# Graph network of four layers: TensorE drains carry three kinds of signals, and the step to the next block of nodes moves to the heads of the passes

## The chip, the cores and the metric

The kernel runs on one core of a Trainium2 chip. The metric is the time of one execution on the device, in microseconds (us), as a median of runs. A profiled execution of the kernel before is at hand as well. A core has TensorE (PE, matmuls; PEld is its loading of weights), VectorE (DVE), ScalarE (ACT), GpSimd (POOL) and SyncE (SP, which here only issues DMAs). Each works through its own list of instructions in order, and they wait for one another by semaphores.

## The reference

6,250 nodes with 64 features each go through four layers over the same 200,000 edges (sorted by destination). Each layer takes the normed and rectified features `h` of the nodes and adds its result to `x`.

```python
h = relu(layernorm(x));  x = x + L0(h, edge_attr, src, dst, W, b)
    # msg = [h[src], edge_attr];  agg = segment_sum(msg, dst);  relu([h, agg] @ W.T + b)
h = relu(layernorm(x));  x = x + L1(...)
    # pre = h[src] @ W_q + h[dst] @ W_k + edge_attr @ W_e;  score = leaky(pre) @ a_w
    # softmax of the scores over each dst;  segment_sum(alpha * (h[dst] @ W_v), dst)
h = relu(layernorm(x));  x = x + L2(...)
    # segment_sum(h[src] * weight, dst)
h = relu(layernorm(x));  x = x + L3(...)
    # attention by relation and rule: q of dst, keys of src; softmax over each dst; segment_sum
```

## The kernel before

The edges are 392 batches of 512 (4 tiles of 128). Each layer is one pass over the batches: `sum0` (layer 0, from about 120 to 2330 us), `score1` (layer 1, 2400 to 4966), `sum2` (layer 2, 4990 to 5665) and `attention3` (layer 3, 5790 to 8236). Between them stand the phases `head`, `middle1`, `middle2`, `middle3` and `end3`, which work on nodes, not on edges. Each pass and each phase is a block of its own with a barrier of all engines behind it (`Phase`, its end at L224, L227 and L230).

In a pass each engine runs its own `pipeline(eng, [(lag, stage), ...])`: in each step it does the listed stages in the order of the list, each for the batch that lies `lag` behind. So the order on an engine is fixed, and an engine that waits in one stage holds up all stages behind it. `done(eng, s, b)` waits until semaphore `s` has counted batch `b`, and `free(eng, s, b, ring)` until it has counted the batch that used the same slot before.

GpSimd gathers the rows of the source nodes by four indirect DMAs for each batch (`gather_stage`, L801) in `sum0` (table `node_rows`; for one batch in eight the rows come from TensorE lookups instead), `score1` (`src_rows`) and `attention3` (`rel_rows`). `sum2` has no gathers: it reads rows that `score1` kept in memory. The gathered rows lie in 8 slots (`ROW_RING`). A slot comes free in `sum0` by `s_sum` (TensorE's sum of the batch, L1119), in `score1` by `s_pre` (VectorE's `join`, L1512).

The stages that the change touches:
- `sum0`, TensorE `sums` (L1119): four matmuls add the rows of a batch into a bank, and the last of them signals `s_sum`. VectorE's `add` (L1168), VectorE's `build` (L1158), ScalarE's `join` (L1080) and GpSimd's gathers wait for it. The lookups (`lookups`, L1127) signal `s_used_dve` and `s_used_act` by their matmuls; VectorE (L1199) and ScalarE (L1097) wait for them.
- `score1`, TensorE `look` (L1488 and L1493) waits for VectorE's `hot` (L882), for `s_score` (VectorE's `scores`, L1527) and for the edge features, and signals `s_looked`. VectorE's `join` (L1512) and SyncE's next loads (L1446) wait for it.
- `score1`, TensorE `spread` (L1390) waits for `s_diag` (ScalarE, L1399) and signals `s_spread`, for which VectorE's `maxima` (L1539) and ScalarE's `spread_stage` (L1399) wait.

```python
pipeline(pe, [(1, look), (6, spread)])
pipeline(dve, [(7, maxima), (4, join), (9, sums), (7, running), (4, leak),
               (7, tops), (0, hot), (7, biases), (4, scores)])
```

VectorE's `scores` is last in its step and TensorE's `look` of the next step waits for a `scores` one step back. Nodes are treated in windows of 128. A pass stands in a loop over windows that here runs once (all instruction counts are 392 or multiples). Behind each pass, a phase `<name>_next` steps `dst_rel`, `dst_pairs`, `window_lane` and `base` to the next window (L910, L915, L918, L934), and the phases between the layers set them back (`reset_windows`, L906, and the copies at L1948, L1950 and L2006).

## Time and profile before

| | |
|---|---|
| runs | 8364.23 us median of 3 (8340.83 to 8364.46) |
| profiled execution | 8303.98 us, span in the trace 8301.9 us |
| busy in the span | PE 62%, PEld 45%, VectorE 55%, ScalarE 51%, GpSimd 60% |
| `sum0`, 120 to 2330 us | 5.6 us for a batch |
| `score1`, 2400 to 4966 us | 6.5 us for a batch |
| `sum2`, 4990 to 5665 us | 1.7 us for a batch |
| `attention3`, 5790 to 8236 us | 6.2 us for a batch |

No engine is busy for much over 60% of the span. The rows below are from the same execution; "idle before" is the time in which an engine stood still ahead of an instruction, and the name behind the arrow is what the profile takes to have ended it ("remote" is a semaphore for which it names no instruction, "issue" is no wait that it shows).

### The profile page before, as it was taken

How to read it: one execution, taken by the hardware profiler on the slowest of the kernel's cores; microseconds unless marked ns; L12 is line 12 of the kernel's file. 1: busy time of each engine (PE TensorE's matmuls, PEld its weight loads, DVE VectorE, ACT ScalarE, POOL GpSimd, SP SyncE). 2: the span in 40 equal slices, each digit the busy share in tenths (PEclk: the TensorE clock that was granted, in tenths of full speed). 3: DMA queues.
4: the chain of work that ended last, by engine and by line, in shares of the span. 5: the costliest groups of instructions: out<-in, count | busy, mean ns of one | idle time of the engine just before them, and what ended most of it. 6: DMA issues, size and time to landing. Idle time of an engine off the chain costs nothing. (4 is left out here: it accounts for less than half of the span.)

```text
span 8301.9 us, 160097 instructions
## 1 busy us (share of the span) xinstructions
PE 5143.2 (62%) x38193; PEld 3732.4 (45%) x38194; DVE 4604.7 (55%) x21263; ACT 4230.9 (51%) x11643; POOL 4975.0 (60%) x5713
## 2 busy tenths in 40 slices
PE   4666666666664444444444458997666666666665
PEld 3555556555552222222222227885444444444443
DVE  5555545555544444444444458996555555555556
ACT  3555555555524444444444448994555555555554
POOL 5555555555536556665655648994566666666563
PEclk8888888888876666766666669998666666666666
DMA  4333323233334444444444447885222222222221
GB/s 117 92 90 89 89 81 95 83 89 88 89 88 134 132 130 133 133 132 132 135 132 130 133 110 238 268 267 206 59 64 65 62 65 64 65 64 64 63 65 42
DMA packets 673099, 908.82 MB, mean 109 GB/s; under 512 B 141462, under 2 KB 430216, under 8 KB 672729
## 3 DMA queue, kind: packets, MB, share of 16 engines
q1 hardware_dynamic: 502654, 605.53, 23.2%
q0 software_dynamic: 168944, 301.30, 15.0%
q8 instruction: 42, 0.69, 0.0%
q14 instruction: 102, 0.84, 0.0%
q10 hardware_dynamic: 1357, 0.47, 0.0%
HBM read 696.57 MB, written 210.28 MB: 109 GB/s over the span
## 5 line engine op out<-in xcount | busy, mean ns | idle before, releaser
L801 POOL DMA_INDIRECT rows<-src_rows,idx_slots x1531 | 1488.2, 972 | 1009.8 <-issue 505.5
L801 POOL DMA_INDIRECT rows<-rel_rows,idx_slots x1531 | 1455.2, 950 | 941.6 <-issue 377.6
L801 POOL DMA_INDIRECT rows<-node_rows,idx_slots x1339 | 1281.4, 957 | 935.2 <-PE bank L1119 342.9
L1399 ACT ACTIVATE onehot<-ident,fresh_slots 128x128 f32<-128x128 f32 x3136 | 998.9, 390 | 1090.5 <-remote 787.6
L1390 PE MATMUL bank<-onehot,ones 128*128 128x512 f32 x1568 | 1279.6, 912 | 4.8 <-ACT onehot L1399 4.8
L1488 PE MATMUL bank<-w_e,edge_in 128*128 128x256 f32 x784 | 410.4, 622 | 1334.0 <-remote 693.2
L1097 ACT ACTIVATE dst_pairs<-pre,minus_node 128x512 bf16<-128x512 int16 x816 | 578.6, 720 | 1096.6 <-remote 649.3
L1488 PEld LDWEIGHTS bank<-w_e,edge_in 128*128 128x128 f32 x784 | 187.0, 285 | 1763.2 <-issue 1173.0
L1127 PE MATMUL bank<-by_chunk,dst_pairs 128*128 128x192 bf16 x6144 | 776.7, 269 | 322.7 <-issue 239.7
L1539 DVE CUSTOM_DVE_ANT_0 onehots<-bank,onehots 128x512 f32<-128x512 f32 x392 | 271.0, 691 | 1132.2 <-remote 823.1
L1127 PEld LDWEIGHTS bank<-by_chunk,dst_pairs 128*128 128x128 bf16 x6144 | 581.8, 108 | 408.8 <-issue 291.6
L1127 PE MATMUL bank<-wide_room,dst_pairs 128*128 128x192 bf16 x3264 | 476.4, 279 | 454.0 <-ACT dst_pairs L1101 303.7
L1696 PE MATMUL bank<-rows,onehot 128*128 128x65 f32 x3136 | 595.5, 351 | 239.5 <-DVE wide_room L1793 179.7
L1199 DVE TENSOR_SCALAR dst_pairs<-pre,node_at 128x512 bf16<-128x512 int16 x1536 | 534.5, 348 | 277.9 <-remote 156.0
L1696 PEld LDWEIGHTS bank<-rows,onehot 128*128 128x128 f32 x3136 | 547.7, 263 | 266.6 <-issue 249.5
L1636 ACT ACTIVATE shrink<-grown 128x1 f32<-128x1 f32 x392 | 80.0, 204 | 1103.0 <-DVE grown L1741 554.2
L1168 DVE TENSOR_TENSOR wide_room<-bank,wide_room 96x128 f32 x392 | 112.3, 286 | 816.4 <-remote 564.4
L1127 PEld LDWEIGHTS bank<-wide_room,dst_pairs 128*128 128x128 bf16 x3264 | 309.6, 110 | 535.8 <-ACT dst_pairs L1101 341.9
L1101 ACT ACTIVATE dst_pairs<-dst_pairs,ones 128x512 bf16<-128x512 bf16 x816 | 542.2, 709 | 1.6
L1651 ACT ACTIVATE onehot<-onehots,edge_in 128x128 f32<-128x128 bf16 x1568 | 503.1, 392 | 19.9
L1318 ACT ACTIVATE onehot<-onehots,edge_scale 128x128 f32<-128x128 bf16 x1568 | 503.0, 392 | 11.6 <-DVE onehots L1373 11.4
L1471 ACT ACTIVATE onehot<-onehots,exp_bias 128x512 bf16<-128x512 f32 x392 | 283.7, 724 | 428.9 <-DVE max_by_chunk L1569 198.8
(309 smaller groups left out, 12039.1 us busy)
## 6 DMA issues: line engine op xcount, KB each, us to landing
edge_in<-dst_line SPq DMA_DIRECT2D x392, 256.0 KB
spill<-rows SPq DMA_DIRECT2D x392, 256.0 KB
rows<-spill SPq DMA_DIRECT2D x392, 256.0 KB, 3.1
hot_rows<-rows SPq DMA_DIRECT2D x98, 712.0 KB
onehots<-hot_rows SPq DMA_DIRECT2D x196, 356.0 KB, 3.5
onehots<-src_low SPq DMA_DIRECT2D x98, 512.0 KB
edge_in<-in_ea_l SPq DMA_DIRECT2D x98, 256.0 KB
edge_in<-in_eaT_l SPq DMA_DIRECT2D x392, 64.0 KB
```

What stands on the lines that cost most here:

```text
L801: pool.indirect_dma_start(out=to[:, b.slot(ROW_RING), g, :], out_offset=None, in_=table, in_offset=bass.IndirectOffsetOnAxis(ap=idx[:, col ...
L1097: act.activation(act_hots[:, n % 2, :], look_in(b), ACT.Square, bias=minus_node[:, n:n + 1]).then_inc(s_square, 1)
L1101: act.activation(act_hots[:, n % 2, :], act_hots[:, n % 2, :], ACT.Relu, scale=-1.0, bias=ones[:, 0:1])\
L1127: last = pe.matmul(look_banks(b)[g // 2][:, at:at + PARTS * D], hot[:, g * P:(g + 1) * P], node_parts(j), start=(j == 0 and g % 2 == 0), s ...
L1199: dve.tensor_scalar(dve_hots[:, n % 4, :], look_in(b), node_at[:, n:n + 1], None, ALU.is_equal)\
L1318: last = act.activation(onehot[:, b.slot(RING), g, :], plain_of(b)[:, g, :], ACT.Copy, scale=edge_scale[:, b.slot(RING), g:g + 1])
L1390: return pe.matmul(bank, ones[:, :], diag[:, b.slot(2), :, :].rearrange("p g e -> p (g e)"), start=start, stop=True)
L1399: last = act.activation(diag[:, b.slot(2), g, :], ident[:, :], ACT.Copy, scale=fresh_slots[:, b.slot(2 * RING), g:g + 1])
L1471: act.activation(exp_out, masked1[:, b.slot(2), :], ACT.Exp, bias=exp_bias[:, slot, :], accum_out=exp_sum[:, slot, :])
L1488: pe.matmul(to, edge_blocks[:, b.slot(RING), :], w1_e[:, :, :].rearrange("p g f -> p (g f)"), start=True, stop=False)
L1651: last = act.activation(weighted[:, b.slot(2), g, :], onehot_b[:, b.slot(ONEHOT_RING), g, :], ACT.Copy, scale=share[:, b.slot(RING), g:g + 1])
L1696: last = pe.matmul(summed, weighted[:, b.slot(2), g, :], rows[:, b.slot(ROW_RING), g, D:2 * D + 1], start=(g == 0), stop=(g == TILES_PER_B ...
```

## The change

Two things are changed. First, at three places the last matmul of a stage no longer carries the signal: a `drain` of TensorE stands behind it and carries it. These are `sums` of `sum0`, `look` of `score1` and `spread` of `score1`, 392 each, 1176 in all. The signals of the lookups in `sum0`, and all of `sum2` and `attention3`, stay on matmuls. Second, the four phases `<name>_next` are gone, and their steps stand at the head of each pass on VectorE (`next_window`). So that the first step gives the first window, the start values are set one window back (`dst_rel` plus 128, `window_lane` and `base` minus 128), and `reset_windows` has three instructions in place of five. TensorE waits for the stepped `base` ahead of its pipeline in `score1` and `attention3`. The diff, cut:

```diff
--- before.py
+++ after.py
@@ -658,10 +658,13 @@
                 c.do(dve.tensor_reduce(n_windows[:, :], base[:, :], AX, ALU.max))
                 c.do(dve.tensor_single_scalar(n_windows[:, :], n_windows[:, :], 1, ALU.add))
                 dve.wait_ge(s_local, 1)
-                dve.tensor_copy(dst_rel[:, :], dst_rel0[:, :]).then_inc(s_set, 1)
-                dve.tensor_copy(base[:, :], base0[:, :]).then_inc(s_set, 1)
+                dve.tensor_single_scalar(dst_rel[:, :], dst_rel0[:, :], float(WINDOW), ALU.add)\
+                   .then_inc(s_set, 1)
+                dve.tensor_single_scalar(base[:, :], base0[:, :], -WINDOW, ALU.add)\
+                   .then_inc(s_set, 1)
                 dve.wait_ge(s_const, 14)
-                dve.tensor_copy(window_lane[:, :], lane[:, :]).then_inc(s_set, 1)
+                dve.tensor_single_scalar(window_lane[:, :], lane[:, :], float(-WINDOW), ALU.add)\
+                   .then_inc(s_set, 1)
                 dve.wait_ge(s_set, 3)
 
                 dve.wait_ge(s_w, 16 * (len(weight_loads) + 3 + TILES_PER_BATCH))
@@ -894,16 +897,14 @@
                                ACT.Copy, scale=-FAR_BELOW, bias=FAR_BELOW).then_inc(s_far, 1)
             return fars
 
-        n_reset = 5
+        n_reset = 3
 
         def reset_windows(pool, s_set):
 
-            for n, (to, of) in enumerate(((dst_rel[:, :], dst_rel0[:, :]),
-                                          (dst_pairs[:, :, 0], dst_rel0[:, :]),
-                                          (dst_pairs[:, :, 1], dst_rel0[:, :]),
-                                          (window_lane[:, :], lane[:, :]),
-                                          (base[:, :], base0[:, :]))):
-                pool.tensor_copy(to, of).then_inc(s_set, 1)
+            for n, (to, of, by) in enumerate(((dst_rel[:, :], dst_rel0[:, :], float(WINDOW)),
+                                              (window_lane[:, :], lane[:, :], float(-WINDOW)),
+                                              (base[:, :], base0[:, :], -WINDOW))):
+                pool.tensor_single_scalar(to, of, by, ALU.add).then_inc(s_set, 1)
                 pool.wait_ge(s_set, n + 1)
 
         def next_places(dve, c):
@@ -918,21 +919,19 @@
             c.do(dve.tensor_single_scalar(window_lane[:, :], window_lane[:, :], float(WINDOW),
                                           ALU.add))
 
-        def windows_loop(name, sweep, steps):
+        def next_window(dve, s_stepped, s_based, steps):
+
+            c = Chain(dve, s_stepped)
+            for step in steps:
+                step(dve, c)
+            dve.tensor_scalar(base[:, :], base[:, :], WINDOW, LAST_BASE, ALU.add,
+                              ALU.min).then_inc(s_based, 1)
+            dve.wait_ge(s_based, 1)
+
+        def windows_loop(sweep):
             windows = nc.values_load(n_windows[0:1, 0:1], min_val=1, max_val=N_PAD // WINDOW + 1)
             with nc.Fori(0, windows):
                 sweep()
-                with Phase(nc, name + "_next") as ph:
-                    s = ph.sem("set")
-                    block = ph.open()
-
-                    @block.vector
-                    def _(dve):
-                        c = Chain(dve, s)
-                        for step in steps:
-                            step(dve, c)
-                        c.do(dve.tensor_scalar(base[:, :], base[:, :], WINDOW, LAST_BASE,
-                                               ALU.add, ALU.min))
 
         def sum_sweep(name):
 
@@ -1116,10 +1116,10 @@
                             done(pe, s_joined, b)
                             free(pe, s_added, b, 2)
                             for g in range(TILES_PER_BATCH):
-                                last = pe.matmul(sum_bank(b), sum_rows[:, b.slot(ROW_RING), g, :],
+                                pe.matmul(sum_bank(b), sum_rows[:, b.slot(ROW_RING), g, :],
                                                  onehots_of(b)[:, g, :],
                                                  start=(g == 0), stop=(g == TILES_PER_BATCH - 1))
-                            last.then_inc(s_sum, 1)
+                            pe.drain().then_inc(s_sum, 1)
 
                         def look_up(b, hot, j):
                             for g in range(TILES_PER_BATCH):
@@ -1213,6 +1213,7 @@
                                     bank[:, 0:2 * PARTS * D].rearrange(
                                         "p (g n d) -> p g d n", n=PARTS, d=D), AX)
                             last.then_inc(s_filled, 1)
+                        next_window(dve, s_stepped, s_based, [next_places])
                         c = Chain(dve, s_parts)
                         for tiles in src_groups:
                             value = of_tiles(normed, tiles)
...
@@ -1490,18 +1494,20 @@
                                       start=True, stop=False)
                             for g in range(TILES_PER_BATCH):
                                 for n, part in enumerate(parts):
-                                    last = pe.matmul(
+                                    pe.matmul(
                                         to[:, g * D:(g + 1) * D],
                                         onehotT[:, b.slot(ONEHOT_RING), g, :], part, start=False,
                                         stop=(g == TILES_PER_BATCH - 1 and n == PARTS - 1))
-                            last.then_inc(s_looked, 1)
+                            pe.drain().then_inc(s_looked, 1)
 
                         def spread(b):
                             done(pe, s_diag, b)
                             free(pe, s_max, b, RING)
-                            spread_scores(pe, b, spread_bank(b)).then_inc(s_spread, 1)
+                            spread_scores(pe, b, spread_bank(b))
+                            pe.drain().then_inc(s_spread, 1)
 
                         fill_table(pe, w1_k, D, s_table, s_took)
+                        pe.wait_ge(s_based, 1)
                         pipeline(pe, [(1, look), (6, spread)])
 
                     @block.vector
@@ -1580,13 +1586,14 @@
                                 ALU.mult, ALU.add).then_inc(s_den, 1)
                         hot = hot_stage(dve, s_line, s_hot, [s_looked, s_far])
 
+                        next_window(dve, s_stepped, s_based, [next_lane])
                         split_table(dve, Chain(dve, s_chain), D, 0, s_table, s_took)
                         pipeline(dve, [(7, maxima), (4, join), (9, sums), (7, running), (4, leak),
                                        (7, tops), (0, hot), (7, biases), (4, scores)])
                         dve.wait_ge(s_bias, N_BATCHES)
                         dve.wait_ge(s_den, N_BATCHES)
                         dve.wait_ge(s_score, N_BATCHES)
-            windows_loop(name, sweep, [next_lane])
+            windows_loop(sweep)
 
         def attention_sweep(name):
 
...
@@ -1795,13 +1804,14 @@
                         build = onehot_b_stage(dve, s_onehot, [s_weighted])
                         hot = hot_stage(dve, s_line, s_hot, [s_found, s_far])
                         dve.memset(rows[:, :, :, 2 * D:2 * D + 1], 1.0).then_inc(s_ones, 1)
+                        next_window(dve, s_stepped, s_based, [next_pairs, next_lane])
                         split_table(dve, Chain(dve, s_chain), D + N_ACTIVE, N_ACTIVE, s_table, s_took)
                         pipeline(dve, [(3, maxima), (3, running),
                                        (3, high), (3, left), (0, hot), (3, middle), (3, low),
                                        (1, scores), (3, take), (3, differ), (5, add), (0, build),
                                        (3, clamp)])
                         dve.wait_ge(s_added, N_BATCHES)
-            windows_loop(name, sweep, [next_pairs, next_lane])
+            windows_loop(sweep)
 
 
 
@@ -2003,10 +2012,8 @@
             def _(act):
                 act.wait_ge(s_diff, 1)
                 act.activation(max_by_chunk[:, :], max_by_chunk[:, :], ACT.Exp).then_inc(s_exp, 1)
-                act.activation(dst_rel[:, :], dst_rel0[:, :], ACT.Copy).then_inc(s_places, 1)
-                for t in range(2):
-                    act.activation(dst_pairs[:, :, t], dst_rel0[:, :], ACT.Copy)\
-                       .then_inc(s_places, 1)
+                act.activation(dst_rel[:, :], dst_rel0[:, :], ACT.Copy, scale=1.0,
+                               bias=float(WINDOW)).then_inc(s_places, 1)
                 act.wait_ge(s_joined, BLOCKS)
                 act.activation(accT[:, :], ones[:, 0:1].to_broadcast([P, N_PAD]), ACT.Copy,
                                scale=0.0).then_inc(s_clear, 1)
```

The instructions of VectorE at the head of `sum0`, before the change (L729 to L732 split the normed features into parts):

```order
L922 TENSOR_LOAD n_windows
L923 UNCONDITIONAL_BRANCH
L1153 UNCONDITIONAL_BRANCH
L729 CAST by_chunk<-by_chunk 128x8x64
L730 TENSOR_TENSOR rel_biases<-by_chunk 128x512
```

The same place after the change:

```order
L932 TENSOR_LOAD n_windows
L933 UNCONDITIONAL_BRANCH
L1153 UNCONDITIONAL_BRANCH
L911 TENSOR_SCALAR dst_rel<-dst_rel 128x1568
L927 TENSOR_SCALAR bases<-bases 1x392
L732 CAST by_chunk<-by_chunk 128x8x64
L733 TENSOR_TENSOR rel_biases<-by_chunk 128x512
```

The step of `dst_rel` and `base` now stands ahead of the first part. VectorE at the end of `sum0`, before the change:

```order
L1168 TENSOR_TENSOR wide_room<-bank,wide_room 96x128
L224 UNCONDITIONAL_BRANCH
L929 UNCONDITIONAL_BRANCH
L910 TENSOR_SCALAR dst_rel<-dst_rel 128x1568
L934 TENSOR_SCALAR bases<-bases 1x392
L224 UNCONDITIONAL_BRANCH
L923 REGISTER_ALU
L923 COMPARE_AND_BRANCH
```

And after it:

```order
L1168 TENSOR_TENSOR wide_room<-bank,wide_room 96x128
L224 UNCONDITIONAL_BRANCH
L933 REGISTER_ALU
L933 COMPARE_AND_BRANCH
L1869 UNCONDITIONAL_BRANCH
L1877 SCALAR_TENSOR_TENSOR x<-bank,x 128x512
```

Both instructions are gone from there, with the branch into the block that held them. VectorE at the head of `attention3`, before the change (L768 and the lines behind it take TensorE's table of keys):

```order
L1704 UNCONDITIONAL_BRANCH
L1797 MEMSET rows 128x32
L768 TENSOR_SCALAR rule_by_chunk<-bank 128x7x4
L729 CAST by_chunk<-bank 128x7x64
L730 TENSOR_TENSOR onehot<-bank,by_chunk 128x448
```

And after it:

```order
L1713 UNCONDITIONAL_BRANCH
L1806 MEMSET rows 128x32
L911 TENSOR_SCALAR dst_rel<-dst_rel 128x1568
L916 CAST dst_pairs<-dst_rel 128x1568 x2
L919 TENSOR_SCALAR window_lane<-window_lane 128x1
L927 TENSOR_SCALAR bases<-bases 1x392
L771 TENSOR_SCALAR rule_by_chunk<-bank 128x7x4
```

Five instructions now stand between the memset and the first use of the table. The matmuls of TensorE stand in the same order before and after.

## Rows read from the trace of the kernel before

**Rows 1.** Windows, one a pass: PE, PEld, DVE, ACT, POOL busy; clock, DMA share, GB/s.

```profile
120.00:2330.00 2210.00, 1457.03 (x12424) 1284.28 (x12424) 1140.24 (x3156) 1142.39 (x1997) 1269.92 (x1327) 0.85 0.31 88
2400.00:4966.00 2566.00, 1192.50 (x6340) 634.45 (x6340) 1202.18 (x7476) 1053.54 (x3136) 1513.60 (x1558) 0.68 0.47 130
4990.00:5665.00 675.00, 658.23 (x7846) 557.20 (x7846) 628.36 (x1576) 638.77 (x1968) 610.88 (x1176) 0.98 0.81 258
5790.00:8236.00 2446.00, 1646.90 (x10584) 1108.38 (x10584) 1373.96 (x8647) 1284.95 (x4312) 1467.55 (x1544) 0.68 0.24 63
```

**Rows 2.** Waits in score1: total us, times, longest.

```profile
DVE onehots L1539 <- remote: 823.1, 168, 7.9
ACT onehot L1399 <- remote: 787.6, 170, 7.5
POOL rows L801 <- issue: 513.8, 1411, 23.6
POOL rows L801 <- DVE pre L1512: 504.2, 147, 6.0
```

**Rows 3.** Timeline of score1, 3500 to 3517 us: start, us, instruction, idle before.

```profile
3504.26 1.10 PE L1390 MATMUL bank<-onehot,ones 128*128 128x512 f32 x2
...
3509.06 0.09 DVE L1527 DVE_READ_ACCUMULATOR2_ANT fresh_slots<- 128x1 f32 x1
...
3512.11 0.95 POOL L801 DMA_INDIRECT rows<-src_rows,idx_slots  x1 [0.30 <-issue]
...
3514.55 1.22 PE L1488 MATMUL bank<-w_e,edge_in 128*128 128x256 f32 x2 [9.19 <-remote]
...
3515.37 1.29 ACT L1399 ACTIVATE onehot<-ident,fresh_slots 128x128 f32<-128x128 f32 x4 [5.85 <-remote]
...
3515.56 0.69 DVE L1539 CUSTOM_DVE_ANT_0 onehots<-bank,onehots 128x512 f32<-128x512 f32 x1 [6.42 <-remote]
```

**Rows 4.** Waits in sum0: total us, times, longest.

```profile
ACT dst_pairs L1097 <- remote: 610.6, 164, 7.9
DVE wide_room L1168 <- remote: 563.1, 202, 4.8
...
POOL rows L801 <- PE bank L1119: 342.9, 102, 8.8
POOL rows L801 <- issue: 327.2, 1049, 2.9
POOL rows L801 <- remote: 255.2, 176, 2.2
```

**Rows 5.** Timeline of sum0, 1000 to 1012 us.

```profile
1002.07 1.04 PE L1119 MATMUL bank<-onehots,rows 128*96 128x128 f32 x8
...
1005.22 0.95 POOL L801 DMA_INDIRECT rows<-node_rows,idx_slots  x1 [0.31 <-issue]
...
1007.84 1.34 ACT L1097 ACTIVATE dst_pairs<-pre,minus_node 128x512 bf16<-128x512 int16 x2 [7.18 <-remote]
```

**Rows 6.** Waits in sum2, the same kind of sum and add.

```profile
DVE wide_room L1384 <- PE bank L1301: 16.4, 50, 1.3
```

**Rows 7.** Timeline of DVE at the ends of the passes.

```profile
2331.46 0.98 DVE L910 TENSOR_SCALAR dst_rel<-dst_rel 128x1568 f32<-128x1568 f32 x1 [2.29 <-PEq L230]
2332.47 0.35 DVE L934 TENSOR_SCALAR bases<-bases 1x392 int32<-1x392 int32 x1
...
8238.14 0.98 DVE L910 TENSOR_SCALAR dst_rel<-dst_rel 128x1568 f32<-128x1568 f32 x1 [1.65 <-PEq L230]
8239.15 2.11 DVE L915 CAST dst_pairs<-dst_rel 128x1568 bf16<-128x1568 f32 x2
...
8242.98 0.14 DVE L2201 MEMSET by_chunk<- 64x100 f32 x1 [1.14 <-PEq L227]
```

**Rows 8.** Timeline behind sum0, and of DVE at the head of attention3.

```profile
2334.00 0.18 POOL L1903 MEMSET max_by_chunk<- 128x99 f32 x1 [19.84 <-POOLq L227]
...
5791.14 0.19 DVE L768 TENSOR_SCALAR rule_by_chunk<-bank 128x28 f32<-128x28 f32 x1 [9.82 <-DMA edge_in<-in_ea_l]
```

More of the change, by code:

```diff
@@ L956, in sweep @@
                     s_marks = ph.sem("marks")
+                    s_stepped, s_based = ph.sem("stepped"), ph.sem("based")
                     block = ph.open()
@@ L1226, in _ @@
                                  unroll=GATHER_UNROLL)
-            windows_loop(name, sweep, [next_places])
+            windows_loop(sweep)
         def kept_sum_sweep(name):
@@ L1384, in add @@
                             dve.tensor_tensor(at, sum_bank(b), at, ALU.add).then_inc(s_added, 1)
+                        next_window(dve, s_stepped, s_based, [next_pairs])
                         pipeline(dve, [(2, pick), (7, add), (2, fold), (3, plain)])
-            windows_loop(name, sweep, [next_pairs])
+            windows_loop(sweep)
         def spread_scores(pe, b, bank, start=True):
@@ L1609, in sweep @@
                     s_ones = ph.sem("ones")
+                    s_stepped, s_based = ph.sem("stepped"), ph.sem("based")
                     block = ph.open()
@@ L1947, in _ @@
             def _(pool):
-                pool.tensor_copy(window_lane[:, :], lane[:, :]).then_inc(s_set, 1)
+                pool.tensor_single_scalar(base[:, :], base0[:, :], -WINDOW, ALU.add)\
+                    .then_inc(s_set, 1)
                 pool.wait_ge(s_set, 1)
-                pool.tensor_copy(base[:, :], base0[:, :]).then_inc(s_set, 1)
-                pool.wait_ge(s_set, 2)
             @block.vector
```

5 lines of the change are left out of this document (added).

## Prediction

> **What bounds the kernel now.** I read the windows of the four passes first. In the pass without gathers, `sum2`, TensorE is busy for 658.2 of 675 us and its granted clock is 0.98 of full speed. In the three passes with gathers no engine comes near that: in `score1` the busiest is GpSimd with 1513.6 of 2566 us, in `sum0` TensorE with 1457 of 2210, in `attention3` TensorE with 1647 of 2446, and the granted clock is 0.68 to 0.85 [rows 1]. So these passes, which hold 7,222 of the 8,302 us, are bound by waiting, and the question is for what.
>
> The table of waits answers for `score1`. VectorE waits 823 us ahead of L1539 (`maxima`) and ScalarE 788 us ahead of L1399, both for a semaphore that the profile does not name ("remote"), and GpSimd waits 504 us in 147 stops for VectorE's L1512 (`join`), besides 514 us of "issue" that is spread over its gathers [rows 2]. GpSimd's own pace is a floor: 1513.6 busy and 513.8 issue are 2,027 us for 392 batches, 5.2 us for each, of the 6.5 that a batch takes.
>
> Then I read the timeline, to see what is late. TensorE's `spread` matmul (L1390) ends at 3505.36, VectorE's last piece of `scores` (L1527) at 3509.15. From then on every engine but GpSimd stands still. GpSimd's last gather of its run starts at 3512.11 and ends at 3513.06. Only after it do TensorE (3514.55, for which the profile says 9.19 us of "remote"), ScalarE (3515.37, 5.85 us) and VectorE (3515.56, 6.42 us) go on, within 1.0 us of each other [rows 3]. What VectorE's `maxima` and ScalarE's `spread_stage` need of TensorE had been done by 3505.36, as far as the modelled end of the matmul can be trusted. I read this as signals that are held up while GpSimd issues gathers and that come when it stops. GpSimd stops because its 8 slots are full, and they come free only through the stages that are held up.
>
> `sum0` shows the same picture. The sum (L1119) ends at 1003.11, GpSimd's run of gathers at 1006.17 (its last starts at 1005.22), and ScalarE's L1097, 7.18 us idle, starts at 1007.84 [rows 5]. The waits are 611 us at L1097, 563 us at L1168 (`add`, which waits for the sums alone), and GpSimd stands 343 us behind L1119 in 102 stops and 255 us behind "remote" in 176 [rows 4]. In `sum2`, where the same kind of `add` waits for the same kind of sum and no gathers run, that wait is 16 us [rows 6]. The contrast of 563 and 16 us is my best evidence that the gathers, and not the sums, make the signal late. That it is the signal, and not the matmul itself, no row shows, since the ends of matmuls are modelled.
>
> **The change, part by part.** *The 1176 drains.* The program has no drain behind a matmul in these passes, so what one costs I bound. Below, it costs nothing: TensorE is idle for 753 of 2210 us in `sum0` and for 1,373 of 2566 us in `score1` [rows 1], and a drain behind the last matmul of a stage mostly stands where TensorE would wait anyway. Above, it keeps the weights of the next matmul from loading under the one before. PEld is busy 1284 us over 12,424 loads in `sum0` and 634 over 6,340 in `score1` [rows 1], 0.10 us each; 1176 of them laid bare are 118 us. I take zero, as the idle time is far larger, and keep the 118 us for the range. Queued behind a drain on TensorE are the lookups (in `sum0`), `spread` (behind `look`) and the next `look` (behind `spread`), and VectorE and ScalarE wait for all three.
>
> The gain hangs on whether a drain's signal comes when the matmuls are done. Its bounds: nothing, if it is held up as they are, and all of GpSimd's stops, 504 us in `score1` [rows 2] and 343 + 255 = 598 us in `sum0` [rows 4]. I size it by stops. In `score1` 392 batches in 147 stops are 2.67 batches for a stop, of 504/147 = 3.43 us. If `s_looked` and `s_spread` come at once, VectorE can do its next step: `join` frees a slot for GpSimd. But TensorE's `look` of the step after waits for VectorE's `scores`, whose signal no drain carries, and rows 3 show TensorE itself waiting 9.19 us though `scores` was done at 3509.15. So each run of gathers grows by one to two batches, not without end. With 1.5 more (my choice), stops fall to 392/4.17 = 94, and 94 x 3.43 = 322 us remain: **182 us gained in `score1`**.
>
> In `sum0` 392 batches in 278 stops are 1.41 for a stop, of 598/278 = 2.15 us. One batch more for each run gives 163 stops and 350 us, 248 us less. But only the sums get drains. The lookups' signals stay on matmuls, and 611 us of ScalarE's waits hang on those [rows 4]; a batch in eight takes its rows from there. I take half, **125 us**. `attention3` keeps its signals, and I take zero for it.
>
> The Trainium skill speaks against the change in two places. "PSUM — Partial Sum Buffer", section "Engine vs sequencer instructions", says that the increment belongs on the matmul that produces, and that a drain waits until the engine is fully idle. "TensorE: Matmul & The Clock Gate", section "Single matmul latency", gives about 175 ns for the way of a matmul's result out of the array, which one that is followed by another hides and an isolated one doesn't; 1176 of them, an estimate from that page, would be some 206 us if none lay beside a wait. No row of the kernel before shows either.
>
> *The four phases.* After `sum0` the phase holds VectorE from 2331.46, and the next one begins at 2334.00 [rows 7, 8]: 2.5 us. After `attention3` it is 8238.14 to 8242.98, 4.8 us [rows 7]. `score1` has one small step of these and `sum2` the large ones, so I take 2 and 4.7 us for them (estimates from these two): 14 us removed. The work comes back at the heads: 0.98 + 0.35 = 1.3 us in `sum0`, the same and 2.11 more in `attention3` and `sum2`, under 1 in `score1` [rows 7], 9 us at most. In `attention3` VectorE waits 9.82 us there anyway [rows 8], so its 3.6 us are hidden. I take **8 us gained**; the bounds are 5 and 14. The casts that `reset_windows` loses lie under longer work of the phases, and count as nothing.
>
> The sum: 8304 - 182 - 125 - 8 = 7989 us against the profiled execution. The median of the runs is 8364.23, 0.73% above that execution, so the forecast in their terms is 7989 x 1.0073 = 8047 us, or **8045 us**.
>
> **The rivals.**
> 1. *Gathers become the bound.* The drains free everything, `scores` included, since VectorE no longer falls idle behind it. Then `score1` loses most of its 504 us and `sum0` most of its 598. For it speaks that GpSimd has no other long wait; against it, TensorE's wait for `scores` in rows 3. With two thirds of both, 8304 - 735 - 8 = 7561, or 7616 us in the runs' terms. Chance 0.14.
> 2. *The signals are not the point.* Whatever is held up is held up for all, `scores` and the lookups too, until GpSimd stops; drains change which wait is named, not its end. Then only the phases count: 8296, or 8356 us. Rows 3 speak for it, since three engines go on together. Chance 0.13.
> 3. *The other side: the drain is held up too, and holds TensorE.* What is late may be the writing of the results into the bank rather than the news of it. A drain then waits as long as VectorE does now, and TensorE, which till now went on with the next stage, stands behind it. (By the PSUM page's rule of the Trainium skill, that a drain waits for the idle engine, this is what would follow.) The place is `look` ahead of `spread` in `score1`, and the sum ahead of the lookups in `sum0`. Each run of gathers then ends half a batch sooner in `score1` (2.17 for a stop: 181 stops, 620 us, 116 more) and 0.2 batches sooner in `sum0` (1.21: 324 stops, 697 us, 99 more). 8304 + 215 - 8 = 8511, or 8573 us. It decides from where a drain stands for more than the time that TensorE would idle anyway. For it speaks that TensorE is the one engine that could run ahead; against it, that in rows 3 TensorE waits for VectorE in any case. The bare cost of the drains (118 us) belongs on this side as well. Chance 0.23.
>
> The forecast itself has 0.50.
>
> **How the numbers follow.** 0.3% is about what a measurement of this kernel can tell from no change, here 25 us. Faster holds the forecast and rival 1, and a little of rival 2: 0.65. Same holds most of rival 2: 0.11. Slower holds rival 3 and the rest: 0.24. The range of the forecast alone is 7,800 (three more batches for a stop in `score1`, all of the 248 us in `sum0`) to 8,270 (half the gain, the drains' 118 us partly paid). For 8 in 10 it must reach to the other cases on both sides: from 7,600, rival 1, to 8,500, which leaves the further part of rival 3 outside.
>
> **What the profile of the changed kernel would show.** If the forecast holds, VectorE's wait at `maxima` in `score1` falls from 823 us to under 500 and that of `add` in `sum0` from 563 to under 250; GpSimd's stops for `join` fall from 147 towards 94; the wait at `look` stays or grows, now as the one that is left; and `attention3` takes 6.2 us for a batch as before. Rival 1 shows a batch of `score1` at 5.2 to 5.5 us. Rival 2 shows the same waits to within a few per cent. Rival 3 shows TensorE's drains taking microseconds and more stops of GpSimd. The phases show as 5 to 14 us less between the last instruction of a pass and the first of the next block. The prediction is wrong in its root if the waits at `maxima` and `add` stay while the drains themselves end at once, for then VectorE waited for something else.

## The result and the profile after

The changed kernel takes 8835.87 us (median of 4 runs, 8820.34 to 8846.87) where the kernel before takes 8360.55 (4 runs): a ratio of 1.0572, 95% interval 1.0545 to 1.0599, or 475 us slower. The forecast was 8045 us.

The windows of the four passes in the changed kernel, with the columns of [rows 1]:

```profile
120.00:2391.00 2271.00, 1448.05 (x12440) 1294.69 (x12440) 1136.98 (x3156) 1144.28 (x1997) 1265.94 (x1327) 0.88 0.30 86
2461.00:5466.00 3005.00, 1438.16 (x6344) 681.96 (x6343) 1186.41 (x7476) 1057.79 (x3136) 1523.14 (x1559) 0.58 0.40 111
5490.00:6162.00 672.00, 656.36 (x7845) 555.48 (x7844) 628.19 (x1579) 635.63 (x1965) 609.66 (x1176) 0.99 0.81 260
6285.00:8758.00 2473.00, 1648.60 (x10389) 1144.77 (x10584) 1367.35 (x8643) 1279.00 (x4312) 1475.19 (x1543) 0.65 0.24 62
```

Layer 1 is 439 us longer (3005 for 2566), layer 0 61, `attention3`, whose batches are as before, 27, and `sum2` 3 shorter. The loss lies in layer 1, where two of the three drains stand. VectorE, ScalarE and GpSimd are busy there within 16 us of what they were before. TensorE is busy for 246 us more with the same matmuls, and its granted clock is 0.58 of full speed instead of 0.68.

The drains, each from the view of its line (`sums` at L1122, `look` at L1501, `spread` at L1507; after the count min/median/max in ns, then first and last start):

```profile
L1122 PEldq DRAIN  x392: 927/3727/23883, 74.6 to 2388.2; - x196
```

```profile
L1501 PEldq DRAIN  x392: 547/1992/13617, 2516.6 to 5447.2; - x196
```

```profile
L1507 PEldq DRAIN  x392: 1070/2050/2895, 2539.3 to 5459.5; - x196
```

With nothing held up, `look`'s drain lasts 1.46 us at most (a run below), so one of 13.6 us has waited for something else than its matmuls. The timeline of layer 1 shows for what. This is a stretch of the changed kernel around one stop of GpSimd, and under it the two drains of `look` that start between 3499 and 3504 us:

```profile
3502.97 1.28 ACT L1402 ACTIVATE onehot<-ident,fresh_slots 128x128 f32<-128x128 f32 x4 [1.06 <-PEq L1507]
...
3503.18 1.19 PE L1492 MATMUL bank<-w_e,edge_in 128*128 128x256 f32 x2 [0.33 <-issue]
...
3508.94 0.95 POOL L804 DMA_INDIRECT rows<-src_rows,idx_slots  x1 [0.30 <-issue]
...
3511.73 0.59 SPq L1450 DMA_DIRECT2D edge_in<-in_eaT_l  x1
...
3511.76 2.05 PE L1393 MATMUL bank<-onehot,ones 128*128 128x512 f32 x2 [6.79 <-issue]
...
3513.86 1.28 ACT L1402 ACTIVATE onehot<-ident,fresh_slots 128x128 f32<-128x128 f32 x4 [7.12 <-PEq L1507]
...
3515.37 1.19 POOL L804 DMA_INDIRECT rows<-src_rows,idx_slots  x1 [5.47 <-DVE pre L1518]
```

```profile
L1501 PEldq DRAIN  x2: 1402/4685/7968, 3499.2 to 3503.6; - x2
```

`look` starts at 3503.18. What `spread` (L1393) needs from ScalarE is ready at 3504.25 (it starts at 3502.97 and takes 1.28 us). Yet `spread` starts only at 3511.76: TensorE stands for 6.79 us behind `look`'s drain, and the profile calls that "issue", since no semaphore is awaited. The drain starts at 3503.6, lasts 7.97 us and so ends at 3511.55, 1.7 us after GpSimd's last gather (which ends at 3509.89). SyncE, which waits for the drain's signal, goes on at 3511.73. ScalarE then waits until `spread` and its own drain are over (3513.86), and GpSimd stands still for 5.47 us until VectorE's `join` has come round. In the kernel before, nothing stands between `look` and `spread`: once ScalarE's part was ready at 3504.25, `spread` could have gone on while `look`'s signal was still out.

The waits of layer 1 in the kernel before that [rows 2] leaves out:

```profile
PE bank L1488 <- remote: 693.2, 104, 10.2
...
PE bank L1488 <- issue: 356.3, 77, 11.0
...
DVE onehots L1539 <- PE bank L1390: 261.5, 112, 8.4
ACT onehot L1399 <- PE bank L1390: 206.9, 76, 10.3
```

The waits of layer 1 in the changed kernel, and below them two of layer 0:

```profile
DVE onehots L1545 <- PEq L1507: 1665.0, 351, 11.7
ACT onehot L1402 <- PEq L1507: 1511.1, 337, 14.4
...
PE bank L1393 <- issue: 1300.3, 384, 13.2
POOL rows L804 <- DVE pre L1518: 849.9, 167, 6.2
...
PE bank L1492 <- issue: 214.6, 383, 9.3
```

```profile
DVE wide_room L1168 <- PEq L1122: 1069.8, 384, 6.3
...
POOL rows L804 <- PEq L1122: 678.0, 329, 7.4
```

The wait at `maxima` was 823 us of "remote" [rows 2] and 262 named for `spread`'s matmul, 1085 together, and is 1665 us now. It is named for the drain of `spread` (L1507), which lasts no longer than its matmuls (2.05 us in the middle, 2.9 at most). That row misleads: the drain named is the last link. TensorE's own waits show what changed. Before, it stood ahead of `look` (L1488: 693 and 356 us are the largest parts, 1334 in all), with `spread` already done. Now it stands for 1300 us ahead of `spread` (L1393) and for 215 ahead of `look` (L1492, 232 with the smaller parts). In all it stands still 194 us longer (1567 us of the window, 1373 before), and above all in another place: when the release comes, `spread` is still to be done. GpSimd's stops in layer 1 went from 504 us in 147 [rows 2] to 850 in 167, in layer 0 from 598 in 278 [rows 4] to 678 in 329.

### The profile page after: what moved, and what is told of

It reads as the page before. It is cut to its first block and busy times, and to the rows that moved or that the text cites. A ratio compares the mean times of both kernels' runs of the same rounds, so it can differ in the third digit from the quotient of the medians.

```text
span 8818.6 us, 160978 instructions
## 1 busy us (share of the span) xinstructions
PE 5385.4 (61%) x37998; PEld 3828.6 (43%) x38194; DVE 4579.4 (52%) x21263; ACT 4226.4 (48%) x11641; POOL 4988.1 (57%) x5708
## 5 line engine op out<-in xcount | busy, mean ns | idle before, releaser
L1393 PE MATMUL bank<-onehot,ones 128*128 128x512 f32 x1568 | 1429.8, 1012 | 1424.0 <-issue 1378.5
L1127 PE MATMUL bank<-by_chunk,dst_pairs 128*128 128x192 bf16 x6144 | 773.5, 280 | 767.8 <-issue 767.4
L1393 PEld LDWEIGHTS bank<-onehot,ones 128*128 128x128 f32 x1568 | 408.6, 290 | 1387.4 <-issue 1351.2
L1127 PEld LDWEIGHTS bank<-by_chunk,dst_pairs 128*128 128x128 bf16 x6144 | 597.2, 111 | 866.3 <-issue 848.8
L1704 PE MATMUL bank<-rows,onehot 128*128 128x65 f32 x3136 | 614.1, 359 | 243.3 <-DVE wide_room L1802 208.6
L1492 PE MATMUL bank<-w_e,edge_in 128*128 128x256 f32 x784 | 431.5, 650 | 232.4 <-issue 214.6
L1101 ACT ACTIVATE dst_pairs<-dst_pairs,ones 128x512 bf16<-128x512 bf16 x816 | 540.7, 707 | 1.6
L1492 PEld LDWEIGHTS bank<-w_e,edge_in 128*128 128x128 f32 x784 | 181.3, 288 | 803.5 <-issue 781.7
L1127 PE MATMUL bank<-wide_room,dst_pairs 128*128 128x192 bf16 x3264 | 480.4, 281 | 76.0 <-ACT dst_pairs L1101 54.2
L1678 PEld LDWEIGHTS bank<-by_chunk,onehots 128*128 128x128 bf16 x3136 | 281.5, 129 | 453.9 <-issue 453.1
```

Source lines behind the costliest of these rows:

```text
L1101: act.activation(act_hots[:, n % 2, :], act_hots[:, n % 2, :], ACT.Relu, scale=-1.0, bias=ones[:, 0:1])\
L1127: last = pe.matmul(look_banks(b)[g // 2][:, at:at + PARTS * D], hot[:, g * P:(g + 1) * P], node_parts(j), start=(j == 0 and g % 2 == 0), s ...
L1393: return pe.matmul(bank, ones[:, :], diag[:, b.slot(2), :, :].rearrange("p g e -> p (g e)"), start=start, stop=True)
L1492: pe.matmul(to, edge_blocks[:, b.slot(RING), :], w1_e[:, :, :].rearrange("p g f -> p (g f)"), start=True, stop=False)
L1678: last = pe.matmul(to, onehotT[:, b.slot(ONEHOT_RING), g, :], part, start=(n == 0), stop=(n == PARTS - 1))
L1704: last = pe.matmul(summed, weighted[:, b.slot(2), g, :], rows[:, b.slot(ROW_RING), g, D:2 * D + 1], start=(g == 0), stop=(g == TILES_PER_B ...
```

## The experiments

Theory A is the third rival of the prediction: a drain waits for whatever holds the signal up, that is until GpSimd's run of gathers ends, and what stands behind it on TensorE waits too. Theory B puts the loss to the moved steps. Theory C is that the cost is the bare emptying of the engine. Theory D doubts that the gathers have anything to do with the late signals. Ratios are to the kernel before on the same chip, with 95% intervals, and times in us are differences of medians. One thing the intervals don't cover: the batches of `attention3` are the same in every run here, and yet they take 2389 to 2441 us from the first to the last add in the eighteen profiles, a spread of 52 us. So a difference of less than some 50 us between two kernels may be clear of 1 and still not be the edit's.

**The steps alone.** The changed kernel with its three signals on matmuls again.

```diff
-                            pe.drain().then_inc(s_sum, 1)
+                            last.then_inc(s_sum, 1)
...
-                            pe.drain().then_inc(s_looked, 1)
+                            last.then_inc(s_looked, 1)
...
-                            spread_scores(pe, b, spread_bank(b))
-                            pe.drain().then_inc(s_spread, 1)
+                            spread_scores(pe, b, spread_bank(b)).then_inc(s_spread, 1)
```

> The changed kernel with all three signals back on the matmuls; only the four phases are gone and the steps stand at the heads. Theory A (the drains make the whole slowdown): 5 to 14 us faster than before, a ratio of 0.998 to 1.000. Theory B (the steps at the heads disturb the passes, for instance by the wait for the stepped base on TensorE): above 1.003.

0.9976 (0.9966 to 0.9985), 8334.41 against 8351.7 us: 17 us faster, near the 14 us that were removed at most, and too little to be put to the steps with certainty. Theory B falls: without the drains nothing is lost.

**The drain of `look` alone, of `spread` alone, and a mute one.** Each on the kernel before.

```diff
-                            last.then_inc(s_looked, 1)
+                            pe.drain().then_inc(s_looked, 1)
```

> The kernel before with the one drain of look in layer 1. In the changed kernel that drain took 1717 us in all, 2.0 us in the middle but 8 us for one in ten, and TensorE's spread stood behind it. Theory A (a drain lasts as long as GpSimd's run of gathers, and TensorE's next stage waits behind it): this drain alone makes most of layer 1's loss, 250 to 440 us, ratio 1.03 to 1.05. Theory C (the loss is the bare cost of emptying the engine, much the same for each drain): 392 of 1176 drains, about a third of 475 us, 100 to 160 us.

1.0189 (1.0170 to 1.0208): 157 us. Its drain is the first of these three rows (`look`'s, `spread`'s alone, the mute one):

```profile
L1497 PEldq DRAIN  x392: 542/5078/12383, 2441.0 to 5125.5; - x196
```

```diff
-                            spread_scores(pe, b, spread_bank(b)).then_inc(s_spread, 1)
+                            spread_scores(pe, b, spread_bank(b))
+                            pe.drain().then_inc(s_spread, 1)
```

> The kernel before with the one drain of spread in layer 1. In the changed kernel it took 2.05 us in the middle and 2.9 at most, about as long as its own matmuls. Theory A: little is lost, as the next look waits for VectorE's scores anyway, and with a prompt signal something may be won: -150 to +60 us. Theory C: 100 to 160 us lost, as for look.

1.0058 (1.0043 to 1.0074), 45 us.

```profile
L1503 PEldq DRAIN  x392: 1100/3717/12517, 2462.5 to 5015.9; - x196
```

```diff
                             last.then_inc(s_looked, 1)
+                            pe.drain()
```

> The kernel before with a drain behind look that carries nothing; the last matmul of look still carries s_looked. It parts the two effects of the drain, holding TensorE and moving the signal. Theory A: TensorE is held as in the run with the look drain, so the loss is the same within 60 us, and the signal of the matmul comes with the drain's end. If the drain's signal were itself the later one, this run would be faster than that with the look drain by more than 60 us.

1.0200 (1.0185 to 1.0216), 169 us, the same as with the signal on the drain (the intervals overlap).

```profile
L1498 PEldq DRAIN  x392: 567/5067/12367, 2450.9 to 5137.3; - x196
```

Read together: by itself each drain is long (3.7 to 5.1 us in the middle, up to 12.5), wherever it stands, so a drain is held up as the signals are. What it costs differs, over three times as much for `look` as for `spread`, which speaks against C's equal prices and for the stage behind the drain. The 45 us of `spread` lie within the spread between kernels named above, the 157 and 169 of `look` well outside. And at `look`, who carries the signal makes no difference: moving it is neither gain nor loss, and holding TensorE is the whole cost. Theory A's 250 us or more for `look` alone was too much.

**The drain of the sums alone.** As above, at `sums` of layer 0.

> The kernel before with the one drain of the sums in layer 0. In the changed kernel it took 1450 us in all, 3.7 us in the middle, with the lookups behind it on TensorE, and the pass ended some 60 us later than before. Theory A (held until GpSimd's run ends): 40 to 90 us lost, all in layer 0. Theory C (bare cost of emptying): about 100 us or more.

1.0010 (0.9999 to 1.0022), 8 us, which can't be told from nothing. Both theories had more. The drain lasts 3.6 us in the middle, and yet TensorE stands ahead of the lookups no longer than before (L1127: 672 us of "issue" and 47 for ScalarE's L1101, where the kernel before has 387 and 282). So the wait behind the drain mostly takes the place of one for ScalarE. That this is why nothing is lost is argued and not shown, and it does not hold on every occasion (further down).

**Both drains of layer 1.** The edits of `look` and `spread` above together.

> The kernel before with the drains of look and of spread in layer 1 and no other. Alone they cost 157 and 49 us, 206 together. The changed kernel lost about 500 us of span with its phases 20 us cheaper and layer 0 about 60 us longer, which leaves some 435 us for layer 1. If the two make it together and more than add (the wait of TensorE at the one delays the other's stage): 380 to 460 us lost, ratio 1.045 to 1.055. If they add: about 206, ratio 1.025, and the rest comes from the steps at the head of layer 1.

1.0440 (1.0413 to 1.0467): 380 us on 8302, against some 200 for the two apart. So they make more together, at the lower edge of what was expected.

**Plain loads for the gathers, without and with the drains.** GpSimd loads 128 fixed rows in each place, in layer 1 only, so the rows are not those of the edges' source nodes.

```diff
+                    if plain:
+                        pool.dma_start(to[:, b.slot(ROW_RING), g, :], table[g * P:(g + 1) * P, :])\
+                            .then_inc(s_rows[b.slot(ROW_RING)], 16)
+                        continue
                     pool.indirect_dma_start(
```

> The kernel before, with GpSimd's gathers of layer 1 replaced by plain loads of 128 fixed rows each, so the rows in layer 1 are other rows. Same bytes, same semaphores, same slots, no index reading. Theory A (GpSimd's gathers hold up what TensorE's matmuls signal): the waits of 823 us at maxima and 788 at ScalarE's spread stage fall below 200 us each and the pass takes under 2000 us, 500 us less or more. Theory D (the signals are late for another reason, as the loads' traffic in memory): the waits stay within a third of what they were.

0.8385 (0.8363 to 0.8406), 6968.34 us against 8302.06: 1334 us less. The window of layer 1, and what is left of the waits ahead of VectorE's `maxima` (here L1543) and ScalarE's spread stage (L1403):

```profile
2443.00:3634.00 1191.00, 788.63 (x6186) 404.72 (x6186) 1127.73 (x7402) 1013.68 (x3123) 809.66 (x1519) 0.98 0.92 275
```

```profile
DVE onehots L1543 <- issue: 19.1, 47, 5.9
...
DVE onehots L1543 <- PE bank L1394: 5.3, 8, 0.8
...
ACT onehot L1403 <- issue: 4.3, 1, 4.3
ACT onehot L1403 <- PE bank L1394: 1.8, 5, 0.4
```

The loads have the same size and the stages are the same, and the waits, 1085 us (823 and 262) and 995 (788 and 207) before, are 24 and 6. VectorE becomes the bound, busy for 1127.73 of 1191 us, and the granted clock is 0.98. Theory D falls, and so does its form that the traffic in memory delays the signals, for the same bytes move here at 275 GB/s in place of 130. Not all of the 1334 us are the hold-up's: GpSimd's floor of 5.2 us for a batch is gone with the gathers as well.

The same with the edits of both drains:

> The same plain loads in layer 1 with the drains of look and spread. Against the plain loads without drains: theory A says that only the bare cost is left, each drain as long as its own matmuls, 0 to 100 us in all against some 430 with gathers. Theory C (the cost is that of emptying, gathers or not): some 400 us here too.

0.8467 (0.8447 to 0.8487), 7027.81 us: 60 us more than without the drains, for 784 of them 76 ns each. Their durations, `look`'s and `spread`'s:

```profile
L1501 PEldq DRAIN  x392: 473/637/1460, 2409.1 to 3637.6; - x196
```

```profile
L1507 PEldq DRAIN  x392: 940/1100/2100, 2421.5 to 3650.0; - x196
```

This is the bare cost, and the longest `look` drain is 1.46 us instead of 13.6. If they cost the same with gathers, 60 of the 380 us are theory C's; at the lower clock there each may cost more, which no run isolates. The Trainium skill ("TensorE: Matmul & The Clock Gate", section "Single matmul latency") gives about 175 ns for the way of a single matmul's result out of the array. The 76 ns measured for a drain are less than half of that; no run shows where the rest is hidden.

**Do the parts add?** The sum so far was 4.4% and the changed kernel had lost 5.7%. All three drains on the kernel before, then the changed kernel with the drain of the sums alone and with the two of layer 1 alone (the edits above, combined):

> The kernel before with all three drains and its four phases kept. The drains of layer 1 alone cost 380 us, that of layer 0 alone 8, and the phases gained 20 by themselves, which adds to 368 where the changed kernel lost 475. If the parts add here, 390 us and a ratio of 1.046 to 1.050, and the other 107 us come from drains together with the steps at the heads. If the drains of the two layers hurt each other, 450 us or more, ratio over 1.053.

1.0464 (1.0446 to 1.0481), 394 us.

> The changed kernel with the drain of the sums in layer 0 alone. Adding gives 20 less and 8 more, 12 us faster than before, ratio 0.998. If the drain of the sums costs more where the steps stand at the heads (layer 0 ended 60 us later in the changed kernel), it is 30 to 60 us slower, ratio 1.004 to 1.007.

0.9989 (0.9979 to 0.9998), 8 us faster, about as adding gives.

> The changed kernel with the drains of look and spread, and the sums of layer 0 signalled by the matmul. Adding gives 380 less 20, 360 us slower than before, ratio 1.043. If layer 1 with the steps at its head is itself slower, 400 us and more; if the 107 us belong to layer 0, 1.043 to 1.046.

1.0371 (1.0354 to 1.0389), 305 us, less than the 360 that adding gives. Nothing here makes the missing 1.3%, so the changed kernel and the three drains were run side by side:

> The changed kernel itself, beside the three drains without the steps. The parts measured so far add to 4.4% at most (three drains 4.6%, steps -0.2%), the changed kernel's first timing gave 5.7%, on a chip where the kernel before took 8360 us and not 8306. If that was the chip or the occasion, 1.042 to 1.048 here. If drains and steps truly make more together, 1.055 to 1.060 here too.

1.0579 (1.0565 to 1.0594), with 8371.01 us for the kernel before.

> The three drains without the steps, again, on the same chip as the changed kernel: 1.046 by its first timing. The difference to the changed kernel is then that of the steps: -0.2% if parts add, +1% if the two make more together.

1.0600 (1.0585 to 1.0614). The very kernel that had 1.0464 beside a kernel before of 8306 us has 1.0600 beside one of 8371. Side by side, the steps make 14 us (0.2%), so they don't make the loss larger. What differs is the price of the drains, by 1.4% between two occasions. The traces show where. These are VectorE's adds of layer 0, with the first and last start behind the durations: the three drains at 1.0464, the same at 1.0600, and, on the same occasion as the latter, a kernel without any drain of TensorE (it has drains of GpSimd in layer 1, and is the second of those further down):

```profile
L1168 DVE TENSOR_TENSOR wide_room<-bank,wide_room x392: 277/287/290, 81.9 to 2344.9; 96x128 f32 x196
```

```profile
L1168 DVE TENSOR_TENSOR wide_room<-bank,wide_room x392: 276/287/290, 81.8 to 2394.2; 96x128 f32 x196
```

```profile
L1170 DVE TENSOR_TENSOR wide_room<-bank,wide_room x392: 276/287/289, 81.9 to 2318.9; 96x128 f32 x196
```

Layer 0 ends 49 us later on the second occasion, and layer 1 takes 84 us more (2940 for 2856 from the first to the last `maxima`). With the drain of the sums, layer 0 is 2251 to 2263 us long in three profiles and 2306 to 2313 in three others, the changed kernel's among them; without it, 2230 to 2263 in all twelve. So that drain, 8 us by itself, lengthens layer 0 by some 70 us on the occasion of the last two rows. Where the price is low, the parts add only to within some 60 us: all three drains cost 394 us, where the 305, the 17 that the steps save and the 8 for the sums make 330. What makes the occasions differ, these runs don't tell.

**Drains of GpSimd.** On the kernel before, behind each batch's four gathers in layer 1.

```diff
                         .then_inc(s_rows[b.slot(ROW_RING)], 16)
+                if pause:
+                    pool.drain()
```

> The kernel before with a drain of GpSimd itself behind each batch's four gathers in layer 1. Theory A1 (what holds the signals up is gathers that GpSimd has in hand, and they come when it has none): a drain every four gathers lets the signals through more often, the runs of 9 gathers become runs of 4, and the waits of 823 us at maxima and 788 at the spread stage fall by a third or more; the time falls by 50 to 300 us unless the drains cost GpSimd as much. Theory A2 (signals come only when GpSimd truly has nothing to do for 1 to 2 us): the drain changes nothing but adds its own time, 0 to 100 us slower.

1.0438 (1.0421 to 1.0456), 8676.16 us. What the waits at `maxima` (L1541) and at the spread stage (L1401) came to, from the table of layer 1's waits:

```profile
POOL rows L801 <- DVE pre L1514: 1020.9, 381, 3.6
DVE onehots L884 <- DMA edge_in<-dst_line: 813.6, 190, 4.9
...
DVE pre L1514 <- DMA rows<-src_rows,idx_slots: 669.4, 287, 4.5
...
DVE onehots L1541 <- issue: 92.4, 142, 3.1
DVE onehots L1541 <- PE bank L1392: 32.4, 34, 1.9
ACT onehot L1401 <- issue: 31.1, 72, 1.9
ACT onehot L1401 <- PE bank L1392: 16.9, 22, 1.5
```

The waits for TensorE fell by far more than a third, as A1 has it, but the time rose: GpSimd now stops 381 times for some 2.7 us, 7.5 us for a batch, and has become the bound itself. VectorE waits for gathered rows (669 us) and for edge data (814) instead, so the short waits at `maxima` alone don't prove that signals come promptly. The trace shows that they do. Of the 240 signals of `spread` that can be matched to their matmul in it, 10 come more than 1 us after the matmul's modelled end. Here `maxima` goes on between two gathers of one run, 0.23 us after that end:

```profile
3524.31 2.06 PE L1392 MATMUL bank<-onehot,ones 128*128 128x512 f32 x2
...
3526.60 0.69 DVE L1541 CUSTOM_DVE_ANT_0 onehots<-bank,onehots 128x512 f32<-128x512 f32 x1 [0.33 <-issue]
...
3526.64 0.95 POOL L801 DMA_INDIRECT rows<-src_rows,idx_slots  x1 [0.30 <-issue]
```

The forecast of that run's time was wrong, that the waits for TensorE would fall was right.

```diff
-                if pause:
+                if pause and b.slot(2) == 1:
```

> The kernel before with a drain of GpSimd behind every second batch's gathers in layer 1. A drain every batch took the waits at maxima from 823 to some 125 us but cost GpSimd 2.65 us for each, 7.5 us a batch. With one for every 8 gathers a batch takes (8 x 1.25 + 2.65) / 2 = 6.3 us where it now takes 6.5: 0 to 80 us faster if that is the bound, up to 60 us slower if the signals held for a run of 8 gathers come on top.

0.9929 (0.9895 to 0.9963), the only one besides the moved steps that is clear of 1 on the good side, with runs from 8253.78 to 8356.28. In its profile layer 1 is no shorter than in the kernel before's, of another occasion (2501 for 2486 us from the first to the last `maxima`), so where the gain lies isn't shown. Its waits:

```profile
DVE onehots L1541 <- remote: 713.1, 187, 8.4
...
DVE onehots L1541 <- PE bank L1392: 173.9, 85, 7.7
```

With eight gathers in a run the waits at `maxima` are back at 887 us, of 1085 in the kernel before. So a drain of GpSimd behind eight gathers doesn't help much, and one behind four does. But it is not the length of the run alone. In layer 0 of the changed kernel 323 of 330 runs have four gathers and end without a drain of GpSimd, and there the signals are held. Such a run, with VectorE's adds, which wait for the drain of the sums:

```profile
1001.58 0.94 POOL L804 DMA_INDIRECT rows<-node_rows,idx_slots  x1 [1.39 <-PEq L1122]
1002.82 1.01 POOL L804 DMA_INDIRECT rows<-node_rows,idx_slots  x1 [0.30 <-issue]
1004.13 1.00 POOL L804 DMA_INDIRECT rows<-node_rows,idx_slots  x1 [0.30 <-issue]
1005.43 0.94 POOL L804 DMA_INDIRECT rows<-node_rows,idx_slots  x1 [0.30 <-issue]
...
1007.67 0.29 DVE L1168 TENSOR_TENSOR wide_room<-bank,wide_room 96x128 f32 x1 [3.35 <-PEq L1122]
```

Counted over that layer, 298 of the sums' drains last over 3 us, and all but 2 of them end behind a run, by 1.1 us in the middle. What the two kinds of runs of four differ in, beside GpSimd's drain, no run isolates.

> The same on top of the moved steps, without drains of TensorE: the gain or loss of the run with GpSimd's drain for every second batch, and 20 us better than that.

0.9977 (0.9966 to 0.9989), no better than the steps alone. Since the two gains did not add, and both are within the spread of `attention3` above or near it, I take neither as shown.

## Why the prediction was wrong

**What bounds the kernel: right.** In the passes with gathers the engines wait for signals of TensorE that come when GpSimd stops. The plain loads, with 24 us for 1085, show it. "When it stops" holds for most of them only. In layer 1 of the kernel before, of the 354 signals of `spread` that can be matched to their matmul in the trace, 235 come more than 1 us after its modelled end, and 188 of these behind a run of gathers; the other 47 come within a long run. One stands just beside [rows 3]:

```profile
3504.60 0.94 POOL L801 DMA_INDIRECT rows<-src_rows,idx_slots  x1 [0.31 <-issue]
...
3505.32 1.28 ACT L1399 ACTIVATE onehot<-ident,fresh_slots 128x128 f32<-128x128 f32 x4 [2.30 <-remote]
...
3505.85 0.95 POOL L801 DMA_INDIRECT rows<-src_rows,idx_slots  x1 [0.30 <-issue]
```

The contrast between layer 0 and `sum2` that the prediction leant on was a good guide.

**The step that failed: "the gain hangs on whether a drain's signal comes when the matmuls are done".** I took it that it does, against my own third rival. The runs show that it doesn't. The drain ends with the hold-up, 1.7 us after the last gather in the rows above, and `look`'s lasts up to 13.6 us with gathers and 1.46 without. With it fell the zero for what a drain holds up on TensorE, since it "mostly stands where TensorE would wait anyway": at `look` it stands ahead of `spread`, which had waited 5 us and now waits 1300, and both drains of layer 1 cost 380 us where 182 were to be gained. The prediction had no evidence that only the news is late, and had said so ("That it is the signal, and not the matmul itself, no row shows"); it should have shifted the chances. The Trainium skill says that a drain waits until the engine is fully idle ("PSUM — Partial Sum Buffer", section "Engine vs sequencer instructions"). The traces agree, if the engine counts as not idle while its signal is out: the mute drain behind `look` lasted up to 12.4 us. They still don't say whether the results in the bank are late or only the acknowledgement.

**The sum.** In layer 1 the forecast had 182 us less; it was 380 more with the two drains in the runs and 439 in the profile of the changed kernel. In layer 0, 125 less; it was 8 more alone (61 in the profile). The steps were put at 8 us less within bounds of 5 and 14; the runs gave 17 and 14, too little above to be told from the variation. Zero for `attention3` was right within 27 us. Zero for the bare cost of a drain was off by 76 ns each, 60 us for 784 where VectorE is the bound; in proportion that is 89 us for 1176, under the bound of 118.

**The rivals.** The third had the mechanism, the place (`look` ahead of `spread`) and the sign, at a chance of 0.23, and 215 us of the 475. In layer 0 its counts were close for the changed kernel (324 stops and 697 us, measured 329 and 678), where the pass is 61 us longer. With the drain of the sums alone they were too high: GpSimd's waits for it were 617 us, 19 more than before, and the run lost 8 us. In layer 1 it had 181 stops of 3.43 us; there were 167 of 5.1. The 20 stops more make 69 of the 346 us, the length of the stops the other 277, since after each release `spread`, its drain, `maxima` and `join` still have to follow one upon the other. That TensorE's 0.58 clock adds to it (`spread`'s drain takes 2.05 us, and 1.10 with the plain loads, where the granted clock is 0.95) the rows suggest and no run isolates. The objection to the rival, that in [rows 3] TensorE waits for VectorE's `scores` anyway, held for one side alone: at `look`, which comes after `scores`, and not at `spread`, which the drain of `look` newly put behind the hold-up. So the sign that the forecast gave for `look`, that its wait stays or grows, failed too: it fell from 1334 us to 232, and 1300 now stand ahead of `spread`. The first two rivals fell. The second had all engines start together whatever the change. The mute drain, which moves no signal and costs 169 us, shows what was missing from it: how much TensorE has already done when the release comes.

**The range.** It ended at 8500 us, below the third rival's own 8573, and the measured 8835.87 lies beyond both.

## What to carry to other kernels

If a signal comes late, ask first whether the engine or only the news is late, and don't put a wait for "all done" in front of work that the engine could have done in the meantime. A drain costs little where nothing holds the engine up (76 ns here). Where something does, it lasts as long as the hold-up, and its price is that of the stage behind it, not of the stage whose signal it carries. Read such a loss from the idle time ahead of the stage behind the drain, since the table of waits names the last link.

## What was new about the hardware

GpSimd's indirect DMAs hold up TensorE's completion: with gathers, mostly 8 or 12 in a run, layer 1 took 2566 us, and with plain loads of the same size 1191 (GpSimd's own floor included). Runs of four hold it up as well in layer 0, where the drain of the sums lasts 3.7 us in the middle, and hardly do in layer 1 when GpSimd drains behind each. The same program differed by 1.4% in the price of its drains between two occasions on which the kernel before differed by 0.8%.
